# One elementwise multiply of the recurrence loop goes from VectorE to GpSimd (recurrent layer with a four-expert feed-forward gate, 8 cores)

## The reference, cut to what matters

```python
xn = _layernorm(x, axis=-1)
# recurrent part
xz = xn @ W_in
xi, z = jnp.split(xz, 2, axis=-1)          # 2048 channels each
proj = xi @ W_xp                           # 1 + 64 + 64 columns
delta = jax.nn.softplus(proj[..., :1])
B = proj[..., 1:65] @ W_B
C = proj[..., 65:] @ W_C
a = jnp.exp(delta * -jnp.exp(A_log))       # one number a token
h = scan(h_t = a_t * h_{t-1} + (B * xi)_t) # along the 4096 tokens
y = (C * h + D * xi) * jax.nn.silu(z)
s = y @ W_out
# gate: four experts with a shared base, the two best of them weighted
g = silu(ffn(xn))
out = x + s * g
```

## Time and profile before

| | |
|---|---|
| median of 3 runs | 5309.18 us (5307.74 to 5311.33) |
| the profiled execution | 5312.87 us, of which its slowest core's span is 5311.3 us |
| stage 1 | up to about 1067 us |
| stage 2 | about 1067 to 2620 us, some 97 us a sub-block |
| loading of stage 3's weights | 2620 to 2743 us |
| stage 3 | 2743 to 5311 us |

### The profile page before, as it was taken

The page is one execution under the profiler, slowest core; times in us unless marked ns, Lnnn a source line. Parts: engine busy times, 40 slices in busy tenths (PEclk is TensorE's granted clock), DMA queues, the critical chain, the costliest instruction groups (busy, mean ns, idle before and its releaser), DMA issues.

```text
span 5311.3 us, 55710 instructions; the slowest of 8 cores (5286.7 to 5311.3 us)
## 1 busy us (share of the span) xinstructions
PE 3217.1 (61%) x20484; PEld 2071.4 (39%) x20484; DVE 2232.1 (42%) x4198; ACT 674.1 (13%) x1364; POOL 304.1 (6%) x175
## 2 busy tenths in 40 slices
PE   1111111164564554655338988888988888988888
PEld 1000000053453443544315545555545555545555
DVE  0333333335445345354314444444454444454444
ACT  0111111111111111111101111111111111111111
POOL 0000000000000000000001111111111111111101
PEclk9555555576776776777657767777767777767777
DMA  9111111100000000000260000000000000000000
GB/s 141 28 29 27 29 27 29 28 17 12 25 13 12 25 13 13 24 13 13 59 116 29 2 28 29 29 29 29 1 29 29 29 29 29 1 29 29 29 29 9
DMA packets 124230, 150.89 MB, mean 28 GB/s; under 512 B 45512, under 2 KB 97081, under 8 KB 121785
## 3 DMA queue, kind: packets, MB, share of 16 engines
q1 hardware_dynamic: 104330, 94.59, 6.1%
q0 software_dynamic: 19632, 52.74, 5.4%
HBM read 140.20 MB, written 43.07 MB: 35 GB/s over the span
## 4 chain that ended last, share of the span: by engine, by line
PE 57%; DVE 12%; DMA 4%; issue 2%; another core or an unknown queue 2%; ACT 1%; POOL 1%; DVEq 0%; SPq 0%; ACTq 0%; POOLq 0%
PE pt L736 11%; PE pt L761 11%; PE pt L754 10%; PE pt L807 9%; PE pt L551 9%; PE pt L642 5%; DMA xnf<-xnT 3%; DVE hch L611 3%; DVE ypre L624 2%; DVE t1b L619 2%; DVE ybf L634 1%; DMA out<-otm 1%; PE pt L590 1%; DVE otm L850 1%
## 5 line engine op out<-in xcount | busy, mean ns | idle before, releaser
L761 PE MATMUL pt<-basebf,idb 128*128 128x256 bf16 x2048 | 719.4, 351 | 0.0
L754 PE MATMUL pt<-llb,Bstk 32*128 32x256 bf16 x2048 | 707.9, 346 | 0.2 <-DVE rbf L774 0.2
L736 PE MATMUL pt<-xnf,WiT 128*128 128x256 bf16 x4096 | 583.0, 316 | 158.7 <-DMA xnf<-xnT 158.7
L642 PE MATMUL pt<-ybf,W_out 128*128 128x256 bf16 x2048 | 260.5, 296 | 572.0 <-DVE ybf L634 572.0
L736 PEld LDWEIGHTS pt<-xnf,WiT 128*128 128x128 bf16 x4096 | 464.2, 114 | 275.4 <-issue 165.8
L551 PE MATMUL pt<-xnf,W_in 128*128 128x256 bf16 x4096 | 480.6, 283 | 129.4 <-DMA xnf<-xnT 129.4
L807 PE MATMUL pt<-hw,WoT 128*128 128x256 bf16 x4096 | 484.4, 284 | 56.1 <-DVE hw L795 56.1
L769 ACT ACTIVATE rbf<-pt 128x1024 bf16<-128x1024 f32 x256 | 262.3, 1025 | 1880.4 <-PE pt L754 1092.5
L551 PEld LDWEIGHTS pt<-xnf,W_in 128*128 128x128 bf16 x4096 | 415.3, 102 | 195.0 <-issue 133.7
L807 PEld LDWEIGHTS pt<-hw,WoT 128*128 128x128 bf16 x4096 | 416.3, 102 | 124.4 <-issue 60.3
L642 PEld LDWEIGHTS pt<-ybf,W_out 128*128 128x128 bf16 x2048 | 215.8, 106 | 617.0 <-issue 576.3
(11 more groups left out here) (104 smaller groups left out, 2101.2 us busy)
## 6 DMA issues: line engine op xcount, KB each, us to landing
xbuf<-x SPq DMA_DIRECT2D x32, 512.0 KB, 3.8
xnf<-xnT SPq DMA_DIRECT2D x32, 512.0 KB, 5.7
sT<-ssb SPq DMA_DIRECT2D x16, 1024.0 KB, 5.3
xin<-x SPq DMA_DIRECT2D x16, 1024.0 KB, 7.2
sin<-sT POOLq DMA_DIRECT2D x16, 1024.0 KB, 6.9
out<-otm SPq DMA_DIRECT2D x32, 512.0 KB, 3.2
W_in<-w_in POOLq DMA_DIRECT2D x1, 8192.0 KB, 58.1
xnT<-xnfm SPq DMA_DIRECT2D x32, 256.0 KB, 2.6
```

What stands on the lines that cost most here:

```text
L642: e.matmul(ps_[:, 0:TP], W_out[:, kc2 * 1024 + mc2 * 128: kc2 * 1024 + (mc2 + 1) * 128], ybf[:, kc2 * TP:(kc2 + 1) * TP], start=(kc2 == 0) ...
L736: bi=bi: e.matmul(PT[bi][:, fcq * TP:(fcq + 1) * TP], WiT[:, kc * 4096 + fc * 128: kc * 4096 + (fc + 1) * 128], xnf2[par][:, kc * TP:(kc + ...
L754: tp=tp, ui=ui: e.matmul(PT[ui][:, fcq * TP:(fcq + 1) * TP], Bstk[32 * ei:32 * ei + 32, fc * 128:(fc + 1) * 128], llb[par][32 * ei:32 * ei ...
L761: p.op("pe", lambda e, fcq=fcq, ui=ui, bb=bb: e.matmul(PT[ui][:, fcq * TP:(fcq + 1) * TP], idb[:], bb[:, fcq * TP:(fcq + 1) * TP], start=F ...
```

## The change

The operation that writes `t1b` is issued on GpSimd's queue in place of VectorE's. Its operands, sizes and types stay. The helper works out the waits anew: the operation now waits for the scan on DVE's semaphore and for `cbf` on ACT's, and L624 waits for it on POOL's semaphore.

```diff
-                        p.op("dve", lambda e, mc=mc, hb=hb, tb=tb: e.tensor_tensor(
+                        p.op("pool", lambda e, mc=mc, hb=hb, tb=tb: e.tensor_tensor(
                             tb[:], cbf[:, mc * TP:(mc + 1) * TP], hb[:],
                             op=ALU.mult),
                             reads=[("cbf", mc), ("hch", mc % 2)],
```

## The result

The changed kernel is slower: 5409.15 us at the median of 10 runs (5374.12 to 5452.32), against 5316.89 us (5307.74 to 5414.81) for the kernel before, 10 runs also. The ratio is 1.0157, with a 95% interval of 1.0118 to 1.0197. Both kernels have runs in which some cores show a lower clock and take longer, and the ratio leaves out only the worst of them: the four runs of the changed kernel whose cores all stay at 0.685 or more take 5374.12 to 5384.24 us, 65 to 75 us above the 5309.18. The ratio stands for about 83 us, with 63 to 105 as its interval.

The account below looks back on a forecast made before the run. DVE alone was taken to set the pace of stage 2's loop; 0.118 us more in each of 256 turns adds 30.2 to the profiled 5312.87 us, giving 5343.1, or 5339 us against the median, range 5316 to 5395.

Parts of the forecast that it names:

- P: Time of POOL's 256-column product in the stage 2 loop, taken as 0.604 us, likeliest between 0.53 and 0.66 us.
- the middle one: Chosen estimate for POOL's product: 0.10 us fixed plus a part by columns, 0.604 us, costing 30 us in all.
- the rival with a larger fixed part: POOL's product has 0.20 to 0.30 us fixed, takes 0.68 to 0.75 us; 5358 to 5376 us; shares chance 0.25.
- the handoff of 0.15 us to POOL: In each loop turn, POOL's product starts 0.15 us after DVE's scan ends, as L795's does after L789 in stage 3.
- so that wait costs nothing while POOL is idle: POOL's wait for `cbf` in the loop is free, because ACT has written all chunks before the sub-block's first scan.
- longer handoffs of the short operations: Sign of a wrong prediction: handoffs in the loop longer than stage 3's 0.15 us to POOL and 0.10 us back.
- nothing else moves: Outside the loop no cost was expected: DMA issue, POOL's next work and stage 3 stay as before.
- 2 us more of standing still starts it from the same level: PE's clock in the L642 stretch still starts from 0.50 after the longer loop, so no cost was counted there.
- a further hold-up or a larger fixed part: Copy and POOL's product exclude each other, or POOL's fixed time is larger; 5353 to 5395 us, chance 0.25.
- Cost by bytes: POOL's product in the loop is priced by bytes moved, 0.88 us, 101 us in all; 5410 us, chance 0.06.
- no change: POOL's product takes 0.45 to 0.53 us, cancelling the gain from the copy; 5299 to 5320 us, chance 0.12.
- faster: POOL's product takes under 0.486 us; at DVE's pace of 0.426 us the kernel takes 5294 us; chance 0.05.

Follow-up runs that it names:

- e5_pool_forms: Kernel before plus eleven extra POOL operations per stage 2 sub-block, results unread; the change's product form took 0.672, 1.160 and 2.137 us for 256, 512 and 1024 columns.
- e1_dve_wait_last: Changed kernel with the waits ahead of POOL's product reordered, DVE's last; ratio to the kernel before 1.0081 (1.0046 to 1.0116).
- e9_half_columns: Changed kernel with POOL's product on only 128 of the 256 columns, the other half left out; ratio to the kernel before 1.0033 (0.9985 to 1.0081).
- e6_change_again: The changed kernel run once more as it is; ratio to the kernel before 1.0131 (1.0099 to 1.0163).
- e4_skew_dve: Kernel before, product on DVE, with L624 of the previous chunk put between scan and copy; ratio to the kernel before 0.9787 (0.9742 to 0.9833).
- e7_every_other_again: Changed kernel with POOL making only the even chunks' products, DVE the odd ones, a repeat run; ratio to the kernel before 1.0046 (1.0021 to 1.0070).

## Why the prediction was right and wrong

**Right.** The direction, the place and the mechanism: DVE's queue puts POOL's product in a row with the scan, DVE's 109 us less of work is worth nothing, and a delay in the loop is given on to PE's wait for `ybf`. The handoff back to DVE is 0.10 us, the copy keeps its 0.154 us, POOL doesn't wait for the copy, and POOL's wait for `cbf` costs nothing. Stage 3 is nearly unchanged: L795 has its 2.115 us, and from the start of the last L642 matmul to the end core 7 takes 2692.8 us instead of 2687.2, core 0 2683.6 instead of 2691.4. Two readings on the way were not exact, without any effect on the sum: the product of the kernel before does have a wait in the program's list, the one for `cbf` on ACT's semaphore, and SBUF-only operations do overlap in the trace before, ScalarE's silu(z) beside the scans, if not on VectorE and GpSimd.

**Wrong: the size.** The forecast was 30 us, the trace has 62.6 us in the loop, and the slowest core has more than that. Two terms of the sum were too small, and a third was put at nothing.

The first is P, "the middle one", 0.604 us. It was mis-sized by the step that took the MEMSET of one column for the fixed part of an operation: 0.10 us, where e5_pool_forms has 0.183. P is 0.672 us, 0.068 more, 17 us over 256 turns. It lies between the forecast's 0.53 to 0.66 us and the 0.68 to 0.75 of the rival with a larger fixed part.

The second is the handoff of 0.15 us to POOL. The step that failed is "so that wait costs nothing while POOL is idle": it looked at the wait for ACT and missed the wait for POOL's own semaphore, which the helper adds because `t1b` was written by POOL two products before. It stands behind the releasing wait and costs 0.06 us, 15 us in all (e1_dve_wait_last took 15.6 us away). 30.2 + 17.4 + 15.4 = 63.0 us, which is the loop's 62.6 within rounding (PE's wait for `ybf` shows 61.4 of it). The prediction had named longer handoffs of the short operations as a sign of being wrong, and it is the sign that showed.

The third was not in the sum: "nothing else moves". From the profile before to that after, PE's waits for `ybf` grow by about 61 us on every core. On core 7 the wait for `xnf` grows as well, from 126.4 to 139.2 us, and L642 is busy for 264.5 instead of 261.2 us: 61.3 + 12.8 + 3.3 = 77 us; its span grows by 75.9 us. On core 0 the wait for `xnf` is 124.0 us in place of 129.4, and stage 2 is 62 us longer. Core 0's span grows by 45.4 us only, as its stage 1 ends 9 us earlier and what follows stage 2 is 8 us shorter: so much can differ between two executions. The time is that of the slowest core.

On the cores whose wait for `xnf` is the same in both profiles to 2 us (1, 2 and 3), the spans differ by 64 to 69 us, and the matmuls of L551 and L642 together are busy for 6 to 9 us more. The prediction had put nothing for them either, with "2 us more of standing still starts it from the same level"; no run tests what lengthens them.

The landing of the loads differs where the wait does (the DMA view of stage 2, bytes of an issue and median us from issue to landing, core 0 and core 7 of the changed kernel):

```profile
xnf<-xnT SPq DMA_DIRECT2D x15, 512.0 KB, 6.5
```
```profile
xnf<-xnT SPq DMA_DIRECT2D x15, 512.0 KB, 7.7
```

The load takes longer on core 7, and so does the write of `sT` just ahead of it, 6.8 us against 5.3. That they meet a neighbouring core's transfers would fit. In e9_half_columns cores 0 and 1 have the long waits together. In every kept trace, all waits above 127 us are on pairs of neighbours (0 and 1, 2 and 3, and so on) whose stage 2 begins at most 4.0 us apart, each by its own span; pairs further apart have 123.8 to 126.8 us. The kernel before has such a pair too, cores 0 and 1 with 129.4 and 128.1 us, and the change touches nothing of stage 1. But no run sets these distances, so the cause is argued and not shown, and whether the change makes such waits longer or more frequent is open. In e6_change_again cores 0, 1, 6 and 7 have such waits (129.9 to 143.3 us), in e4_skew_dve none has (124.0 to 127.7).

The other ratios don't bear out a cost of the change outside the loop: e1_dve_wait_last has 43 us where the wait for `ybf` grows by 46, e7_every_other_again 24 where it grows by 33.5. What the ratio's 83 us have beyond the 71 of the two profiled executions, no trace here shows.

**The range.** By the ratio the kernel takes 1.0157 x 5309.18 = 5393 us, just within the range's upper end of 5395. The median of its 10 runs, 5409 us, lies outside. The time falls into the span of the rival "a further hold-up or a larger fixed part" (5353 to 5395 us, chance 0.25), and that is partly luck. No hold-up by the copy is seen. The fixed part is larger, but 0.183 us and not 0.20 to 0.30, and P by itself would cost 48 us, 5357 us. The rest of the time comes from the wait that stands last and from what lies outside the loop, which neither the forecast nor a rival had. The same luck keeps the time inside the range. Cost by bytes, no change and faster were rightly held unlikely. e9_half_columns puts the point of no loss at P = 0.43 us with the waits as they are; the prediction had 0.486 us, without the extra wait.

## What to carry to other kernels

An operation that moves to another engine is priced by what follows it in the old engine's queue: if the next operation there needs its result, nothing overlaps, and the price is its time on the new engine plus two handoffs, minus its old time and waits. Take the waits for this from the program's list, all of them and in their order, not from another operation's handoff; and put the wait that releases last. Before offloading work from a loop with such dependences, shift the dependent operation by one turn: here that alone, with everything on DVE, made the kernel 2.1% faster, where the offload made it 1.6% slower.

## What the runs showed of the hardware that I had not expected

- GpSimd's two-input product costs 0.183 us and 1.91 ns a column with a bfloat16 operand, 1.67 ns with float32 alone: the wider type is the faster one (1.892 against 2.120 us for 1024 columns). The estimate that the prediction drew from the Trainium skill (GPSIMD Engine Reference, "Performance versus the Vector engine"), 0.615 us for float32, was met by the float32 form (0.613 us), but its 2.6 cycles, 2.17 ns, a column were not; the change's own form, with a bfloat16 operand, took 0.672 us.
- Of a VectorE and a GpSimd operation that each read two operands in SBUF, the one that comes second is held up in part: 0.41 us on an operation of 0.48, 0.35 to 0.45 on a scan of 0.74, beside a product of 0.67; 0.09 on the product behind an operation of 0.45. The Trainium skill (SBUF — State Buffer, "Who interferes with whom") lets such pairs contend and the second wait for the first's whole length; the traces agree on the contention and show less than the whole. The one-column copy inside SBUF didn't contend at all: 0.154 us for the copy and 0.672 for the product beside it, as each takes alone.
- A wait that is already met, behind the one that releases, costs 0.06 us on POOL's queue (0.21 us from scan's end to product against 0.15 in e1_dve_wait_last).
- Consecutive VectorE operations whose waits are already met overlap by about 0.08 us each, where an unmet wait leaves 0.10 us between them, so that an independent operation between a result and its use was worth 0.45 us a turn in e4_skew_dve.
